# A bound and a skipped key in the second stage's row gathers of a two-layer graph network

## The chip, the cores and the metric

The kernel runs on one core of one Trainium2 chip. The metric is the device time of one execution in microseconds (us). The unchanged kernel took 4383.87 us as the median of 3 runs (4382.24 to 4384.48).

## The reference

N = 12500 nodes with D = 256 features (float32). Of the edge lists `src` and `dst`, 100000 drawn pairs stand in both directions (200000 edges) and 12500 self-loops are added; all 212500 are sorted by `dst`.

```python
# layer 1 (GIN with batch norm)
agg = segment_sum(x[src], dst, N)
z = (1 + eps_gin) * x + agg
z = relu(z @ W1 + b1) @ W2 + b2
z = (z - mean(z, 0)) * rsqrt(var(z, 0) + 1e-5) * gamma + beta
x = layernorm(x + (z + x))
# layer 2 (weighted graph convolution)
support = segment_sum(edge_weight[:, None] * x[dst], src, N)
x = layernorm(x + relu(support @ weight))
```

The first layer sums by `dst`, by which the edges are sorted. The second sums by `src`, by which they are not sorted.

## The kernel before, in words

The nodes are tiles of 128 rows (98 of them), the edges are pairs of chunks: a pair is 256 edges, 831 pairs in all. The function `gnn` holds one block of code for each engine; they work at the same time and meet at semaphores.

**First stage** (to about 2160 us of the span). POOL fetches the rows of x by indirect DMA, one DMA for 128 edges (`gather`, L552), into a ring of 32 pairs. DVE makes one-hot matrices from `dst`; PE multiplies the ring's rows by them and sums a node tile in PSUM, then the two dense layers follow. Beside this work the edges are sorted into 49 buckets of 256 nodes of `src` for the second stage: DVE works out each edge's place, PE packs the edges (`pack`, L1366) into runs of 64 slots, each slot a key and a weight. A slot that no edge takes holds key 0 and weight 0. ACT stores the runs in `stage_dram`. Self-loops don't go to a bucket; their weights go into a diagonal.

A **key** is `dst * 256 + (src mod 256)`: the row to fetch and the place in the bucket. The buckets' lists stand in a DRAM tensor `lists` of (key, weight), 4 + 4 bytes an entry. At the start of the kernel SP fills all of `lists` from the SBUF tile `zero_row` with 17 DMAs of 128 KB (L443), after a wait on `s_zero`, which DVE's `memset` of the tile raises (L653). `zero_row` is read as (key, weight) pairs, so that every entry begins as key 0, weight 0.

**Between the stages** (about 2160 to 2329 us) the batch norm and the first layer norm are applied, and x1 is written to `x1_dram` (12544 rows of 1 KB). POOL waits for the 17 fills and writes the runs to their places in `lists` by 47 indirect scatters (L590), in an order in which each run's empty slots are overwritten by the next run of its bucket; what is left of them stands behind a bucket's last entry. Each bucket is taken up to a whole number of pairs. POOL reads the lists back, 128 entries a row (L607), DVE takes the keys apart (L1138 to L1142: cast to integer, shift by 8 for the row to fetch, mask with 255 for the place), PE turns them round and ACT copies the result to `srcT` (indices), `dstT` (places) and `wT` (weights).

**Second stage** (from about 2329 us). POOL runs `rounds2` turns over the ring. For every two pairs there is an `If` on the number of pairs, a wait for the ring's places on `s_added2`, and four calls of `gather2` (L618), each an indirect DMA of 128 rows of x1. SP counts the landed rows (`s_landed2`, wait at L528) and loads the next indices (L518). DVE makes a weighted one-hot of 128x256 for each chunk (L1154: place equal to the node, times the weight), PE multiplies and adds (L1493), two matmuls for each chunk of 128 entries, one for each node tile of the bucket, then the diagonal's part (L1514), the transposes (L1523), the dense layer (L1533), and DVE and ACT do the last layer norm; ACT stores the result.

The DMA instructions of POOL are executed by POOL: the profile shows each as an instruction with a duration of its own, and the landing of the rows apart from it.

The function of the second stage's gather before the change (L615 to L618):

```python
            def gather2(q, c):
                nc.gpsimd.indirect_dma_start(
                    out=ring[:, q, c, :], out_offset=None, in_=x1_dram,
                    in_offset=bass.IndirectOffsetOnAxis(ap=idx[:, q, c:c + 1], axis=0)).then_inc(s_row2[q // TWO], 16)
```

and the loop that calls it:

```python
            with pool.Fori(0, rounds2) as r:
                for h in range(2):
                    pool.wait_ge(s_idx2[h], r * 16 + 16)
                    stand(pool)
                    for q in range(h * HALF, (h + 1) * HALF, TWO):
                        ...
                        with pool.If(r * RING + q < pairs2):
                            pool.wait_ge(s_added2, r * RING + q + 2)
                            stand(pool)
                            for b in range(TWO):
                                for c in range(2):
                                    gather2(q + b, c)
```

Of the kernel before, what the change touches and what calls it, by code (L numbers as in the profile page):

```python
# [6 lines left out]
P = 128  # L7
# [7 lines left out]
TWO = 2  # L15
# [14 lines left out]
ALONE = 2 * TWO + BATCH  # L30
SLOTS = 64
BIG = 1 << 20
IN_RANGE = "the table's entries are clamped to the pairs of a sweep when they are computed"
IN_RANGE2 = "the buckets' chunks are counted from the edges, and all edges fill no more than these pairs"
NORM_EPS = 1e-5
# [19 lines left out]
def gnn(nc, x, src, dst, edge_weight, w1, b1, w2, b2, gamma, beta, eps_gin, w3, lists, stage_dram, z_dram, x1_dram, out):  # L55
# [7 lines left out]
    NT = -(-N // P)  # L63
# [21 lines left out]
    with ctx:  # L85
        def sb(name, shape, dt):
            return ctx.enter_context(nc.sbuf_tensor(name, shape, dt))

        def sem(name):
            return ctx.enter_context(nc.semaphore(name))  # L90
# [70 lines left out]
        zero_row = sb("zero_row", [P, D], f32)  # L161
        all_ones = work[:, 3200:3200 + P]
        idx = sb("idx", [P, RING, 2], i32)
# [178 lines left out]
        s_zero = sem("s_zero")  # L342
# [11 lines left out]
        s_row2 = [sem(f"s_row2_{g}") for g in range(RING // TWO)]  # L354
# [22 lines left out]
        def entry(eng, j):  # L377

            _, values = nc.values_load_multi_w_load_instructions(  # L379
                table[0:1, ds(j, 1), :].rearrange("a t f -> a (t f)"), engines=[eng.engine], min_val=0, max_val=MOST,  # L380
                skip_runtime_bounds_check_because=IN_RANGE)
            return values

        def entry2(eng, j):

            _, values = nc.values_load_multi_w_load_instructions(
                table2[0:1, ds(j, 1), :].rearrange("a t f -> a (t f)"), engines=[eng.engine], min_val=0, max_val=ROWS,
                skip_runtime_bounds_check_because=IN_RANGE2)
            return values
# [21 lines left out]
        def _(sp):  # L411
# [26 lines left out]
                sp.dma_start(idx[:, begin:(h + 1) * HALF, :], srcT[:, begin:(h + 1) * HALF, :]).then_inc(s_idx[h], 16)  # L438

            sp.dma_start(x_pair[:, 0, :, :], x[0:2 * P, :].rearrange("(t p) d -> p t d", p=P)).then_inc(s_x_pair, 16)  # L440
            sp.wait_ge(s_zero, 1)
            for b in range(ZEROS):
                sp.dma_start(lists[b * P * P:(b + 1) * P * P, :].rearrange("(p n) f -> p (n f)", p=P),  # L443
                             zero_row[:, :]).then_inc(s_zero_rows, 16)
# [93 lines left out]
        def _(pool):  # L538
            nc.gpsimd.memset(src_i[:, NB - 1, :], 0).then_inc(s_fill, 1)
            nc.gpsimd.memset(dst_i[:, NB - 1, :], BIG).then_inc(s_fill, 1)  # L540
            nc.gpsimd.memset(next_i[:, NB - 1, :], BIG).then_inc(s_fill, 1)
            nc.gpsimd.memset(w_f[:, NB - 1, :], 0.0).then_inc(s_fill, 1)
# [63 lines left out]
            for b in range(BLOCKS):  # L606
# [3 lines left out]
                    in_offset=bass.IndirectOffsetOnAxis(ap=chunk_row_i[:, b:b + 1], axis=0)).then_inc(s_rows2, 16)  # L610
# [6 lines left out]
            def gather2(q, c):  # L617
                nc.gpsimd.indirect_dma_start(  # L618
                    out=ring[:, q, c, :], out_offset=None, in_=x1_dram,
                    in_offset=bass.IndirectOffsetOnAxis(ap=idx[:, q, c:c + 1], axis=0)).then_inc(s_row2[q // TWO], 16)  # L620

            with pool.Fori(0, rounds2) as r:
                for h in range(2):
# [3 lines that stand above are left out]
                        if q == AHEAD:  # L627
                            pool.wait_ge(s_list2, N_LIST2)
# [6 lines that stand above are left out]
# [3 lines left out]
        def _(dve):  # L638
# [10 lines left out]
            def edge_dmas(count):  # L649
                rows, rest = divmod(count, PAIR)  # L650
                return 16 * ((rows // P > 0) + (rows % P > 0) + (rest > 0))

            nc.vector.memset(zero_row[:, :], 0.0).then_inc(s_zero, 1)  # L653
            dve.wait_ge(s_src, edge_dmas(E))
            nc.vector.tensor_copy(src_f[:, :, :], src_i[:, :, :]).then_inc(s_cast, 1)
            dve.wait_ge(s_iota, 6)
# [101 lines left out]
            def after(k, n):  # L758

                dve.wait_ge(s_sort, k * (MEMBER_OPS + PLACE_OPS) + n)  # L760
                stand(dve)

            def members(k):
# [6 lines left out]
                nc.vector.tensor_scalar(local_i[:, :], src_k, BUCKET - 1, None, ALU.bitwise_and).then_inc(s_sort, 1)  # L770
                nc.vector.tensor_scalar(pad[:, :], dst_k, float(BIG), None, ALU.is_ge).then_inc(s_sort, 1)
                after(k, 3)
# [118 lines left out]
            def ones_of_tile(j, bank):  # L891

                new, head, m4, m2, _, _, _, shared, off, sweep = entry(dve, j)
                counted = sweep * RING + off
                base = tile_base[:, j:j + 1] if isinstance(j, int) else tile_base[:, ds(j, 1)]

                def equal(to, at, n):
                    at = nc.s_assert_within(at, 0, ROWS - n, skip_runtime_bounds_check_because=IN_RANGE)
                    return nc.vector.scalar_tensor_tensor(  # L899
                        out=to.rearrange("p b c n -> p (b c) n"),  # L900
                        in0=p_iota.unsqueeze(1).to_broadcast([P, 2 * n, P]), scalar=base,
                        in1=dstT[:, ds(at, n), :].rearrange("p b c -> p (b c)").unsqueeze(2).to_broadcast([P, 2 * n, P]),
                        op0=ALU.add, op1=ALU.is_equal)

                if not (isinstance(j, int) and j < 2):
                    dve.wait_ge(s_acc, j - 1)
                    stand(dve)
                equal(shared_of[bank], shared, 1).then_inc(s_onehot, 1)
                with dve.If(new < m4):
                    with dve.Fori(new, m4, 2 * TWO) as p:  # L910
                        for b in range(0, 2 * TWO, TWO):
                            dve.wait_ge(s_added, p + counted + (TILE_ONES + b - TWO))
                            stand(dve)
                            equal(loop_of[:, b:b + TWO], p + b, TWO).then_inc(s_onehot, TWO)
                with dve.If(m4 < head):
                    dve.wait_ge(s_added, m4 + counted + (TILE_ONES - TWO))
                    stand(dve)
                    equal(loop_of[:, 0:TWO], m4, TWO).then_inc(s_onehot, TWO)
                equal(heads_of[bank], head, BATCH)
                equal(last_of[bank], m2, 1).then_inc(s_onehot, TILE_ONES - 1)  # L920
# [310 lines left out]
        def _(pe):  # L1231
# [37 lines left out]
            def sum_tile(j, bank, others):  # L1269

                new, head, m4, m2, end, low, rep, _, off, sweep = entry(pe, j)
                first = sweep * RING
                counted = first + off
# [606 lines left out]
```

## Time and profile before

| what | value |
|---|---|
| median of 3 runs | 4383.87 us (4382.24 to 4384.48) |
| the profiled execution's own time | 4377.4 us |
| its span | 4374.5 us |
| PE busy | 3432.7 us (78%) |
| DVE busy | 2605.9 us (60%) |
| ACT busy | 411.9 us (9%) |
| POOL busy | 3195.1 us (73%) |
| DMA | 540.19 MB, mean 123 GB/s |
| mean granted TensorE clock | 0.903 of full speed |

How to read it: busy time is the time in which an engine has an instruction in work; register, branch and semaphore instructions are not counted. PE is TensorE, DVE is VectorE, ACT ScalarE, POOL GpSimd, SP SyncE. PEld is the weight load that goes with a matmul. An engine's name with a q (SPq, PEq) is its sequencer. L618 is line 618 of the kernel. "<-issue" is idle time in which the engine waited for nothing that the profile shows. The profiled execution is one run of its own, 6.5 us shorter than the median of the three.

### The profile page before, as it was taken

Reading aid. Unit: us, or ns where it says so; the run is one execution under the profiler, and the core shown is the slowest. Engines: PE = TensorE matmul, PEld = TensorE weight load, DVE = VectorE, ACT = ScalarE, POOL = GpSimd, SP = SyncE. Lnnn points to the kernel's source line nnn. Section 1 sums busy time; section 2 is a strip of 40 time slices with the busy share of each in tenths; the row PEclk is TensorE's granted clock in tenths of the full one; section 3 lists DMA queues with packets and bytes.
Section 4 is the critical chain, followed back from the end, with each engine's and each line's share of the span. In section 5 each row is a group of like instructions: output and inputs, shape, how many; then the busy total and the mean of one; then the engine's idle time right before and its main releaser. Section 6 shows DMA issues by size and latency. Waiting matters only on the chain.

```text
span 4374.5 us, 69588 instructions
## 1 busy us (share of the span) xinstructions
PE 3432.7 (78%) x16131; PEld 2823.7 (65%) x16132; DVE 2605.9 (60%) x5746; ACT 411.9 (9%) x1055; POOL 3195.1 (73%) x3456
## 2 busy tenths in 40 slices
PE   2788787877778787877636888888888888888887
PEld 2666676766666676766435666676666666666666
DVE  3888787877878787877474344344344344343343
ACT  0000000000000000000151000000000000000001
POOL 6777777777777777777345777777777777777775
PEclk7888888888888898889758999999999999999998
DMA  5344444444444444444583344434434344434343
GB/s 146 112 123 116 121 118 118 118 119 120 116 121 116 121 115 121 118 119 119 161 292 111 113 115 120 119 115 120 120 115 120 117 118 119 120 114 120 114 120 99
DMA packets 305380, 540.19 MB, mean 123 GB/s; under 512 B 85290, under 2 KB 197790, under 8 KB 305326
## 3 DMA queue, kind: packets, MB, share of 16 engines
q0 software_dynamic: 159424, 434.52, 34.5%
q10 hardware_dynamic: 89348, 67.77, 5.0%
q1 hardware_dynamic: 56554, 37.24, 2.9%
q8 instruction: 26, 0.43, 0.0%
q14 instruction: 28, 0.23, 0.0%
HBM read 489.80 MB, written 46.88 MB: 123 GB/s over the span
## 4 chain that ended last, share of the span: by engine, by line
POOL 34%; issue 27%; DVE 24%; DVEq 6%; PE 3%; DMA 2%; ACT 1%; POOLq 1%; ACTq 1%; SPq 0%; PEldq 0%
POOL ring L618 32%; DVE work L887 5%; DVEq L379 5%; DVE slot_is L881 3%; DVE work L784 2%; DVE ps L809 2%; DVE place_f L813 2%; POOL ring L552 1%; PE ps L1493 1%; DVE ones_sb L899 1%; DVE work L884 1%; DMA x_dram<-ring 1%; PE ps L1283 1%; DMA ring<-x_dram,idx 1%; DVE zstats L926 1%
## 5 line engine op out<-in xcount | busy, mean ns | idle before, releaser
L552 POOL DMA_INDIRECT ring<-in_x,idx x1664 | 1586.4, 953 | 503.7 <-issue 473.3
L618 POOL DMA_INDIRECT ring<-x_dram,idx x1612 | 1524.1, 945 | 521.0 <-issue 489.5
L1493 PE MATMUL ps<-ring,work 128*128 x6448 | 1527.1, 392 | 334.3 <-SPq L528 332.1
L1493 PEld LDWEIGHTS ps<-ring,work 128*128 128x128 f32 x6448 | 1221.7, 194 | 625.0 <-issue 465.6
L1154 DVE TENSOR_SCALAR work<-ps,dstT,wT 128x256 f32<-128x256 f32 x1612 | 741.8, 534 | 1136.0 <-PE ps L1493 1065.7
L1283 PE MATMUL ps<-ring,ones_sb 128*128 x3324 | 899.2, 418 | 133.4 <-DVE ones_sb L899 71.4
L1283 PEld LDWEIGHTS ps<-ring,ones_sb 128*128 128x128 f32 x3324 | 676.2, 210 | 286.1 <-issue 186.3
L899 DVE SCALAR_TENSOR_TENSOR ones_sb<-ps,tile_base,dstT 128x256 f32<-128x256 f32 (+1 forms) x294 | 316.1, 1103 | 219.2 <-issue 205.7
L1366 PEld LDWEIGHTS ps<-work 128*128 128x128 f32 x3384 | 414.6, 191 | 14.6 <-DVE work L887 2.3
L1366 PE MATMUL ps<-work 128*128 128x128 f32 x3384 | 415.8, 274 | 1.4 <-DVE work L887 1.4
L1293 PE MATMUL ps<-ring,ones_sb 128*128 x384 | 152.7, 536 | 233.8 <-DVE ones_sb L899 217.5
L884 DVE TENSOR_TENSOR work<-ps,current 128x768 f32<-128x768 f32 x282 | 266.6, 946 | 0.0
L887 DVE TENSOR_TENSOR work<-slot_is,ps 128x768 f32<-128x768 f32 x282 | 265.6, 942 | 0.0
L1293 PEld LDWEIGHTS ps<-ring,ones_sb 128*128 128x128 f32 x384 | 88.0, 254 | 264.1 <-issue 252.5
L1623 ACT ACTIVATE z_pair<-ps,cols 128x256 f32 (+1 forms) x98 | 41.2, 471 | 1496.6 <-DVE zstats L926 1451.9
L1784 ACT ACTIVATE work<-ps 128x512 f32<-128x512 f32 x49 | 29.3, 597 | 1446.9 <-PE ps L1523 1446.9
L881 DVE TENSOR_TENSOR slot_is<-ps,current 128x384 f32<-128x384 f32 x282 | 154.8, 549 | 6.7
L590 POOL DMA_INDIRECT lists<-work,target x47 | 45.5, 967 | 113.2 <-DMA lists<-work,target 71.9
L809 DVE TENSOR_TENSOR ps<-ps,work 128x588 f32<-128x588 f32 x141 | 109.7, 778 | 21.4 <-DVE place_f L813 0.5
L813 DVE TENSOR_REDUCE place_f<-ps 128x12 f32<-128x588 f32 x141 | 108.7, 771 | 20.6
L1346 PE MATMUL ps<-hidT,w2s 128*128 128x256 f32 x392 | 115.5, 424 | 3.8 <-ACT hidT L1613 3.8
L1450 PE MATMUL ps<-ident,ones_sb 128*128 128x128 f32 x196 | 48.0, 426 | 83.8 <-DVE ones_sb L1077 68.9
(244 smaller groups left out, 2160.2 us busy)
## 6 DMA issues: line engine op xcount, KB each, us to landing
ring<-in_x,idx POOLq DMA_INDIRECT x1664
ring<-x_dram,idx POOLq DMA_INDIRECT x1612, 2.7
z_dram<-z_pair ACTq DMA_DIRECT2D x49, 256.0 KB, 3.1
ones_sb<-x_dram ACTq DMA_DIRECT2D x49, 256.0 KB
ring<-z_dram SPq DMA_DIRECT2D x24, 512.0 KB, 6.0
ring<-in_x SPq DMA_DIRECT2D x24, 512.0 KB, 7.0
x_dram<-ring ACTq DMA_DIRECT2D x24, 512.0 KB, 4.3
out<-ones_sb ACTq DMA_DIRECT2D x48, 256.0 KB
```

The source lines that it names most:

```text
L379: _, values = nc.values_load_multi_w_load_instructions(table[0:1, ds(j, 1), :].rearrange("a t f -> a (t f)"), engines=[eng.engine], min_va ...
L552: nc.gpsimd.indirect_dma_start(out=ring[:, q, c, :], out_offset=None, in_=x, in_offset=bass.IndirectOffsetOnAxis(ap=idx[:, q, c:c + 1], ax ...
L618: nc.gpsimd.indirect_dma_start(out=ring[:, q, c, :], out_offset=None, in_=x1_dram, in_offset=bass.IndirectOffsetOnAxis(ap=idx[:, q, c:c + ...
L881: nc.vector.tensor_tensor(slot_is[:, q % 2, :, :], p_iota[:, 0:SLOTS].unsqueeze(1).to_broadcast([P, WIDTH, SLOTS]), current[:, 1, mine].un ...
L884: nc.vector.tensor_tensor(of_run[:, q, :, :], p_iota.unsqueeze(1).to_broadcast([P, WIDTH, P]), current[:, 0, mine].unsqueeze(2).to_broadca ...
L887: nc.vector.tensor_tensor(values[:, q, :, :, :], slot_is[:, q % 2, :, :].unsqueeze(3).to_broadcast([P, WIDTH, SLOTS, 2]), p_packed[:, :, m ...
L899: return nc.vector.scalar_tensor_tensor(out=to.rearrange("p b c n -> p (b c) n"), in0=p_iota.unsqueeze(1).to_broadcast([P, 2 * n, P]), sca ...
L1154: last = nc.vector.tensor_scalar(to[:, b, c, :], bucket_nodes, dstT[:, ds(at + b, 1), c], wT[:, ds(at + b, 1), c], ALU.is_equal, ALU.mult)
L1283: last = nc.tensor.matmul(wide, ones_of[:, b, c, :], summands[:, ds((p + b) & (RING - 1), 1), c, :].rearrange("p a d -> p (a d)"), start=F ...
L1293: nc.tensor.matmul(wide, shared_of[bank][:, 0, c, :], summands[:, ds((new + (RING - 1)) & (RING - 1), 1), c, :].rearrange("p a d -> p (a d)"),
L1366: last = nc.tensor.matmul(p_pack, of_run[:, q, c, :], values[:, q, c, :, :].rearrange("p n f -> p (n f)"), start=(q == 0 and c == 0), stop ...
L1493: last = nc.tensor.matmul(to[:, t * D:(t + 1) * D], ones_of[:, b, c, t * P:(t + 1) * P], ring[:, ds((p + b) & (RING - 1), 1), c, :].rearra ...
```

## The change

The fill of `lists` begins with a key beyond all nodes, 2^23 (row 2^23 / 256 = 32768), at weight 0: `zero_row` is written by two strided memsets in place of one, and SP waits for both. The second stage's gathers get a bound, the last row of `x1_dram` (12543), and indices above it are passed over without an error; nothing is written to the ring's row for them. The first stage's gathers, the scatters and the gathers of the lists stay as they are.

```diff
+NOBODY = 1 << 23
...
-            sp.wait_ge(s_zero, 1)
+            sp.wait_ge(s_zero, 2)
...
             def gather2(q, c):
                 nc.gpsimd.indirect_dma_start(
                     out=ring[:, q, c, :], out_offset=None, in_=x1_dram,
-                    in_offset=bass.IndirectOffsetOnAxis(ap=idx[:, q, c:c + 1], axis=0)).then_inc(s_row2[q // TWO], 16)
+                    in_offset=bass.IndirectOffsetOnAxis(ap=idx[:, q, c:c + 1], axis=0),
+                    bounds_check=NT * P - 1, oob_is_err=False).then_inc(s_row2[q // TWO], 16)
...
-            nc.vector.memset(zero_row[:, :], 0.0).then_inc(s_zero, 1)
+            nc.vector.memset(zero_row[:, :].rearrange("p (n f) -> p n f", f=2)[:, :, 0], float(NOBODY)).then_inc(s_zero, 1)
+            nc.vector.memset(zero_row[:, :].rearrange("p (n f) -> p n f", f=2)[:, :, 1], 0.0).then_inc(s_zero, 1)
```

## Rows read from the trace of the kernel before

**Rows 1.** Busy time by stretch (start:end, length, then each engine), whole span

```profile
100.00:2160.00 2060.00, 1650.59 (x8488) 1389.57 (x8487) 1620.74 (x3295) 163.60 (x522) 1545.29 (x1703) 0.87 0.42 118
2160.00:2330.00 170.00, 67.47 (x286) 54.60 (x284) 111.39 (x394) 89.84 (x177) 57.78 (x60) 0.56 0.80 264
2400.00:4374.00 1974.00, 1642.85 (x7067) 1322.74 (x7067) 803.46 (x1883) 148.80 (x338) 1470.22 (x1556) 0.98 0.40 117
```

**Rows 2.** The chain that ended last, shares by engine and by line

```profile
POOL 34%; issue 27%; DVE 24%; DVEq 6%; PE 3%; DMA 2%; ACT 1%; POOLq 1%; ACTq 1%; SPq 0%; PEldq 0%
POOL ring L618 32%; DVE work L887 5%; DVEq L379 5%; DVE slot_is L881 3%; DVE work L784 2%; DVE ps L809 2%; DVE place_f L813 2%; POOL ring L552 1%; PE ps L1493 1%; DVE ones_sb L899 1%; DVE work L884 1%; DMA x_dram<-ring 1%; PE ps L1283 1%; DMA ring<-x_dram,idx 1%; DVE zstats L926 1%
```

**Rows 3.** Groups on POOL: count, busy us, mean ns, idle before and its releasers

```profile
L552 POOL DMA_INDIRECT ring<-in_x,idx x1664 | 1586.4, 953 | 503.7 <-issue 473.3 <-PE ps L1283 12.1 <-DMA idx<-in_src 4.1
L618 POOL DMA_INDIRECT ring<-x_dram,idx x1612 | 1524.1, 945 | 521.0 <-issue 489.5 <-PEq L1556 30.3 <-PE ps L1493 1.2
L590 POOL DMA_INDIRECT lists<-work,target x47 | 45.5, 967 | 113.2 <-DMA lists<-work,target 71.9 <-DMA work<-stage_dram 39.4 <-issue 1.8
...
L607 POOL DMA_INDIRECT work<-lists,chunk_row_i x14 | 13.6, 974 | 10.0 <-DMA lists<-work,target 6.0 <-issue 4.0
...
L544 POOL IOTA part_i<- 128x1 int32 x1 | 0.1, 123 | 0.1
```

**Rows 4.** Waits from 2329 us on: total us, times, longest us

```profile
DVE work L1154 <- PE ps L1493: 1065.7, 117, 22.8
POOL ring L618 <- issue: 489.5, 1607, 0.3
...
PE ps L1493 <- SPq L528: 332.1, 306, 5.6
```

**Rows 5.** POOL's timeline at the stage's beginning: start us, duration us

```profile
2329.10 0.94 POOL L618 DMA_INDIRECT ring<-x_dram,idx  x1 [30.29 <-PEq L1556]
2330.35 0.94 POOL L618 DMA_INDIRECT ring<-x_dram,idx  x1 [0.30 <-issue]
2331.60 0.95 POOL L618 DMA_INDIRECT ring<-x_dram,idx  x1 [0.30 <-issue]
2332.85 0.95 POOL L618 DMA_INDIRECT ring<-x_dram,idx  x1 [0.30 <-issue]
2334.10 0.95 POOL L618 DMA_INDIRECT ring<-x_dram,idx  x1 [0.30 <-issue]
```

**Rows 6.** Chain at the end of the span: start us, us, what

```profile
4341.70 0.94 POOL ring L618
4342.64 0.30 issue
4342.95 3.57 DMA ring<-x_dram,idx
4346.55 0.32 issue
4346.87 3.72 PE ps L1493 x16
...
4370.10 1.09 ACT ones_sb L1795 x2
```

**Rows 7.** Busy time of the gathers' stretch: PE, PEld, DVE, ACT, POOL, clock, DMA share

```profile
2329.00:4344.00 2015.00, 1681.08 (x7235) 1353.72 (x7236) 829.74 (x1932) 142.14 (x324) 1524.06 (x1612) 0.98 0.40 117
```

**Rows 8.** Timeline of the first 30 us: DVE's first two instructions, SP's fill

```profile
0.87 0.27 DVE L653 MEMSET zero_row<- 128x256 f32 x1 [0.73 <-PEq L1860]
...
8.68 1.09 DVE L655 CAST ring<-ring 128x1792 f32<-128x1792 int32 x1 [7.53 <-DMA ring<-in_src]
...
20.16 9.08 SPq L443 DMA_DIRECT2D lists<-zero_row  x17
```

**Rows 9.** The gathers of line 618: ns min/median/max, and us to landing

```profile
L618 POOL DMA_INDIRECT ring<-x_dram,idx x1612: 942/946/958, 2329.1 to 4342.9; - x180
...
DMA to landing us min/median/max: 2.6/2.7/3.9
```

**Rows 10.** POOL's DMA queue: packets, MB, share of 16 engines' span

```profile
q0 software_dynamic: 159424, 434.52, 34.5%
```

## The prediction

> **What bounds the kernel now.** I read the table of stretches first. From 2330 us on the second stage runs at one mix to the end, and the span splits into 2160 us of first stage, 170 us between, and this last part [rows 1]. The diff touches gathers of this last part only, so that part decides. The chain that ended last gives POOL's line L618, which is the second stage's gather, 32% of the span, the largest share by far, and "issue" 27% [rows 2].
>
> Next, POOL's own groups. L618 is 1612 gathers of 945 ns each, 1524.1 us, and the idle time before them is 489.5 us of "issue" [rows 3]. The waits show that 1607 of the 1612 gathers waited for nothing that the profile shows, never more than 0.3 us, while PE waited 332.1 us for landed rows and DVE 1065.7 us for PE [rows 4]. So POOL feeds everybody and is fed late by nobody. The single gathers show the beat: one starts every 1.25 us from 2329.10 [rows 5] to 4342.95 [rows 6]. 4343.9 - 2329.1 = 2014.8 us, and / 1612 = 1.250 us per gather, with no gap in between. **Whatever the change does to one gather's time on POOL is multiplied by 1612**: 1 ns is 1.6 us. PE is busy 1681 us of these 2015 us, DVE 830, and the DMA engines have a share of 0.40 [rows 7], so none of them limits, and a POOL that is faster by a few per cent would still be the bound.
>
> What is left after the last gather is some 30 us of landing, sums and norms [rows 6], which the change doesn't touch but for the landing.
>
> **The change, part by part.**
>
> *The fill's two memsets.* Before, one memset of 128x256 at 0.87 us, 272 ns; then DVE stands until the edges land at 8.68 us. SP asks for the fill only at 20.2 us [rows 8]. Two strided ones of half the size each, even at 272 ns apiece, end before 1.5 us. Cost 0: hidden under DVE's wait of 7.5 us; without that cover it would be 0.3 us. SP waits for a count of 2 in place of 1, true 18 us before it asks; behind that wait stand only the 17 fills, the same in number and size. POOL waits for all the fills ahead of its first scatter, in the stretch from 2160 us on [rows 1], long after.
>
> *The key.* Keys become whole numbers by the same casts, shifts and transposes: nothing added. The padding's weight stays 0, so what lies in the ring from earlier is multiplied by 0; PE and DVE do the same work.
>
> *How many rows are passed over.* 1612 gathers of 128 entries are 206336. The reference draws 200000 edges (the 12500 loops go another way, as a diagonal); counted by bucket on the drawn lists, 199986 of them are no loops, so 6350 entries are padding. Not all keep the new key: a sorted run is written in pieces of 64 slots, and its empty slots hold key 0, a valid index. Following the runs of the last groups, 2167 padding entries at the buckets' ends get key 0 from a run's tail and 4183 keep the new key. These 4183 (2.0%) lie in 55 of the 1612 gathers; 19 gathers are passed over as a whole. The other 1557 gathers only carry the bound.
>
> *What passing over saves.* No row shows a gather with fewer rows, so bounds: a gather's 945 ns over its 128 rows is 7.4 ns, so at most 4183 x 7.4 = 31 us; at least 0, if a row left out takes POOL as long as a row described. POOL's smallest instruction, over 128x1, is 123 ns [rows 3], so some of the 945 is fixed: (945 - 123) / 128 = 6.4 ns, 27 us. I take 10 us, nearer to the lower end, since the gathers take 942 to 958 ns whatever their indices are [rows 9], padding chunks included, and since an index left out must still be read and judged. The Trainium skill speaks against the saving here ("DMA: Bandwidth & Descriptors", section "Anatomy of one DMA — SWDGE (gpsimd) path"): generating descriptors is a small part, and many can be emitted before the incremental cost shows; by it the saving would be about 0.
>
> *The DMA side.* 4183 rows of 1 KB are 4.3 MB less of 434.52 MB on the software queue [rows 10]. At a share of 0.40 this frees nothing that is waited for. The last gather took 3.57 us to land [rows 6] against a median of 2.7 us [rows 9], and its bucket ends in padding: at most 0.9 us gained, inside the 10 us.
>
> *What the bound costs on the sequencer.* If a register has to be loaded per gather, it falls in the time in which POOL works at the gather before. Each fourth gather already has a comparison, an addition and a wait ahead of it, and the gaps are 0.30 us there too [rows 4, 5]. So 0; without that cover, no row prices it.
>
> *What the bound costs in the gather itself.* This is the term that decides, and no row of before has a bound. Lower end: 0, if every index is compared today anyway or the comparison fits in free slots (I see no way for it to gain on a gather that leaves nothing out). Upper end: a pass of its own over the 128 indices, the price of POOL's smallest instruction, 123 ns. Nearest rows: the kernel's other forms of this same instruction, the scatter at 967 ns and the gather of the lists' chunks at 974 ns against 945 [rows 3]: another form of the work differs by 22 to 29 ns. I take 22 ns, of the group with more members.
>
> **Sum.** 1612 x 22 ns = +35.5 us, less 10 us: +25.5 us. The profiled execution took 4377.4 us (span 4374.5), so 4402.9; the median of the runs shown is 6.5 us above it, so **4409 us** (+0.6%).
>
> **The rivals.** A measurement of this kernel can tell about 0.2% (8.8 us) from no change.
>
> *A, the forecast: the check costs some tens of ns per gather, more than the skipping gives back.* For it: every ns counts 1612 times, from 12 ns up it loses more than 0.2% (12 x 1.612 - 10 = 9 us), and POOL now works from index to descriptor in 7.4 ns, so that any further step per index shows. Against: the step may run in parallel. Chance 0.36, of which 0.05 ends within 0.2%.
>
> *B, nothing moves.* The compare is free and leaving out saves nothing, or the bound isn't acted on at all (the change would not do what it says; a key of 2^23 is row 32768, beyond the 12544 rows). For it: the durations lie within 16 ns and show no dependence on the indices [rows 9]. 4384 us. Chance 0.29.
>
> *C, faster.* The check is free and a row left out saves its share: 27 to 31 us, with the tail up to 0.9 us more: 4353 to 4357 us; with a third of it, 4374. It needs a check under about 10 ns and a saving per row above 2.1 ns (8.8 / 4183). For it: POOL is the bound with no cover at all, so that each saved ns counts in full. Against: 1557 gathers pay, 55 earn. Chance 0.22.
>
> *D, clearly slower: judging each index is a separate step in POOL.* Its place is each gather of L618; its price is from 123 ns (a pass, above) to 822 ns (the whole present work of an index done twice, 945 - 123), thus 1612 x 0.123 - 10 = +188 us, 4572 us, up to +1315 us, about 5700 us. PE doesn't cover any of it, since it waits for POOL already. It decides from 12 ns on. Against: a loop at 7.4 ns per row leaves little room for such code to be slow. Chance 0.13. The Trainium skill has a rule of this kind ("GPSIMD Engine Reference", section "Elementwise — side-by-side cycle accounting"): data-dependent branching on this engine costs about 12 cycles per element; at the 1.2 GHz of the example there that would be an estimated 1.28 us per gather and over 6400 us. No row here shows it; 7.4 ns per row with an index read in it speak against it having applied so far.
>
> **How the numbers follow.** The likeliest case is A, 4409. Faster: C but for 0.01 within 0.2%, so 0.21. Same: B 0.29, 0.05 of A, 0.01 of C: 0.35. Slower: 0.31 of A and D's 0.13: 0.44. The range begins at 4354, nearly the full saving of C, and goes to 4550, beyond A with 100 ns per gather (+151 us, 4535); most of D and the last of C are left out, 0.12 together. As both signs hold weight: A's own range is 4385 to 4470.
>
> **What would show it.** In the changed kernel's profile L618's mean must be read: 967 ns or so by A with the beat at 1.27 us and the same 0.30 us of issue; 945 by B; by C 945 in most gathers and a lower minimum, in the 55 with padding; by D 1068 or more. The beat times 1612 must give the change of the span; if the mean stays and the gap grows, the cost is the sequencer's and my cover was wrong. The packets and MB of the software queue must fall by 4.3 MB, or the bound isn't acted on. The first stage (L552 at 953 ns, until 2160 us) must stay as it is. The forecast is wrong if the mean of L618 stays within 5 ns of 945, or goes beyond 1040.

## The result and the profile after

The changed kernel takes **4465.75 us** (median of 4 runs, 4462.17 to 4468.01) against 4383.2 us before (4 runs): a ratio of 1.0187 with a 95% interval of 1.0173 to 1.0202. It is 82.5 us slower. The direction was forecast, and the cause by name; the size was not: the sum had come to 25.5 us more. The profiled execution took 4462.17 us, with a span of 4459.1 us. Four of the experiments (`r3_bound_only`, `r3_hoist`, `e7_first_stage`, `e6_err`) ran beside a kernel before of 4376.94 us, as here, and all others beside one of 5424 to 5501 us, slowed, at a mean granted clock of about 0.82 in place of 0.90; each time is compared with the kernel before beside it.

POOL's groups on the changed kernel (line numbers have moved by one: L619 is L618 of before, L553 is L552) answer to [rows 3]:

```profile
L619 POOL DMA_INDIRECT ring<-x_dram,idx x1612 | 1612.9, 1001 | 521.1 <-issue 489.7 <-PEq L1559 30.5 <-PE ps L1496 0.9
L553 POOL DMA_INDIRECT ring<-in_x,idx x1664 | 1587.6, 954 | 504.3 <-issue 472.8 <-PE ps L1286 12.9 <-DMA idx<-in_src 3.9
```

The second stage's gather has gone from a mean of 945 to 1001 ns; the first stage's, which the diff leaves alone, from 953 to 954. The idle time before the 1612 gathers is the same to 0.1 us. The list of that line, which answers to [rows 9], shows what was added and how even the step is:

```profile
L619 POOLq MOVE  x1612: 29/29/29, 2327.2 to 4414.6; - x180
L619 POOL DMA_INDIRECT ring<-x_dram,idx x1612: 995/1002/1016, 2328.0 to 4430.6; - x180
```

The bound is a constant in the source and a register in the program: POOL's sequencer loads it anew for each gather, 29 ns. The shortest of the 1612 gathers is 995 ns long, the longest before was 958: every gather has become longer, also the 1557 that pass nothing over. The timeline (answers to [rows 5]) has the new beat with the old gap:

```profile
2328.02 1.01 POOL L619 DMA_INDIRECT ring<-x_dram,idx  x1 [30.47 <-PEq L1559]
2329.34 1.01 POOL L619 DMA_INDIRECT ring<-x_dram,idx  x1 [0.31 <-issue]
2330.65 1.00 POOL L619 DMA_INDIRECT ring<-x_dram,idx  x1 [0.30 <-issue]
```

The last gather starts at 4430.58 and takes 1.00 us, so the beat is (4431.58 - 2328.02) / 1612 = 1.305 us against 1.250: 55 ns. **Where the time came from:** 1612 x 55 = 88.7 us in the second stage; the stage began 1.1 us earlier; and the tail behind the last gather, 30.6 us before, is 27.5 us. 88.7 - 1.1 - 3.1 = 84.5 us; the spans differ by 84.6. Most of the shorter tail can be named on the chain that ended last, which answers to [rows 6]:

```profile
4430.58 2.27 DMA ring<-x_dram,idx
4432.89 0.32 issue
4433.21 3.72 PE ps L1496 x16
...
4440.21 1.96 PE ps L1536 x8
```

The last gather's rows landed after 2.27 us in place of 3.57; by a count on the drawn lists, 114 of its 128 entries are passed over. This 1.3 us is all that the passing over gave: in the four experiments beside 4376.94 us the last landing takes 3.58 to 3.62 us in the three kernels that keep key 0, and 2.27 us in the one with the new key. The next 1.6 us are in a group of eight matmuls of the dense layer, 1.96 us in place of 3.54; it is 1.96 us with the bound alone as well, so it has nothing to do with the passed rows, and its cause is open. The rest of the machine had slack, as said (the row answers to [rows 7]):

```profile
2328.00:4432.00 2104.00, 1681.42 (x7237) 1350.85 (x7238) 832.43 (x1931) 142.14 (x324) 1612.92 (x1612) 0.98 0.37 111
```

PE's 1681 us of work and DVE's 832 now spread over 2104 us. At the start, the two memsets are as cheap as forecast and lie in the same wait of DVE [rows 8]:

```profile
L444 SPq DMA_DIRECT2D lists<-zero_row x17: 428/461/660, 21.2 to 29.6; - x17
L655 DVE MEMSET zero_row<- x1: 165/165/165, 0.9 to 0.9; 128x128 f32 x1
L656 DVE MEMSET zero_row<- x1: 165/165/165, 1.0 to 1.0; 128x128 f32 x1
```

**Did it pass rows over?** The page's line of DMA packets and that of POOL's queue, changed kernel:

```profile
DMA packets 305382, 536.89 MB, mean 120 GB/s; under 512 B 86080, under 2 KB 198596, under 8 KB 305327
...
q0 software_dynamic: 159424, 431.21, 33.4%
```

434.52 - 431.21 = 3.31 MB, or 3232 rows of 1 KB (0.01 MB of rounding is 10 rows). So it did, but fewer than the 4183 that I had counted. A second count on the drawn lists that puts every run at its place in the order of the scatters gives 3241 entries with the new key (3.32 MB), in 55 gathers, none of them wholly passed over. The first count followed only the empty slots behind the last runs. The runs of the first 23 groups are laid right-aligned, with their empty slots in front, and those of the next bucket reach back into the last chunk of a padded bucket: not all empty slots that are left stand behind a bucket's last entry, as the words on the kernel before had it. The number of packets, 159424, is unchanged [rows 10]: a row that is passed over does not shorten the queue's list, it makes a packet small.

### The profile page after: what moved, and what is told of

The parts are those of the page before. It is cut to its first block, busy times and chain, and to the rows that moved or that the text cites. A ratio compares the mean times of both kernels' runs of the same rounds, so it can differ in the third digit from the quotient of the medians.

```text
span 4459.1 us, 71201 instructions
## 1 busy us (share of the span) xinstructions
PE 3438.7 (77%) x16131; PEld 2824.9 (63%) x16132; DVE 2613.1 (59%) x5747; ACT 411.8 (9%) x1055; POOL 3285.3 (74%) x3456
## 3 DMA queue, kind: packets, MB, share of 16 engines
q0 software_dynamic: 159424, 431.21, 33.4%
HBM read 489.80 MB, written 46.88 MB: 120 GB/s over the span
## 4 chain that ended last, share of the span: by engine, by line
issue 34%; POOL 30%; DVE 23%; DVEq 6%; DMA 2%; PE 2%; POOLq 2%; ACT 1%; ACTq 0%; SPq 0%; PEldq 0%
POOL ring L619 27%; DVE work L890 5%; DVEq L380 4%; POOL ring L553 3%; DVE slot_is L884 2%; DVE work L787 2%; DVE ps L812 2%; DVE place_f L816 2%; DVE ones_sb L902 1%; DMA x_dram<-ring 1%; DVE work L887 1%; PE ps L1286 1%; POOLq L619 1%; PE ps L1496 1%; DVE zstats L929 1%
## 5 line engine op out<-in xcount | busy, mean ns | idle before, releaser
L619 POOL DMA_INDIRECT ring<-x_dram,idx x1612 | 1612.9, 1001 | 521.1 <-issue 489.7
L553 POOL DMA_INDIRECT ring<-in_x,idx x1664 | 1587.6, 954 | 504.3 <-issue 472.8
L1496 PE MATMUL ps<-ring,work 128*128 x6448 | 1526.8, 391 | 421.2 <-SPq L529 419.5
```

The source lines that it names most:

```text
L553: nc.gpsimd.indirect_dma_start(out=ring[:, q, c, :], out_offset=None, in_=x, in_offset=bass.IndirectOffsetOnAxis(ap=idx[:, q, c:c + 1], ax ...
L619: nc.gpsimd.indirect_dma_start(out=ring[:, q, c, :], out_offset=None, in_=x1_dram, in_offset=bass.IndirectOffsetOnAxis(ap=idx[:, q, c:c + ...
L1496: last = nc.tensor.matmul(to[:, t * D:(t + 1) * D], ones_of[:, b, c, t * P:(t + 1) * P], ring[:, ds((p + b) & (RING - 1), 1), c, :].rearra ...
```

## The experiments

**The bound alone.** The lists are filled with key 0 as before, only the bound is added:

```diff
-                    in_offset=bass.IndirectOffsetOnAxis(ap=idx[:, q, c:c + 1], axis=0)).then_inc(s_row2[q // TWO], 16)
+                    in_offset=bass.IndirectOffsetOnAxis(ap=idx[:, q, c:c + 1], axis=0),
+                    bounds_check=NT * P - 1, oob_is_err=False).then_inc(s_row2[q // TWO], 16)
```

> The kernel before with the bound alone: the lists are filled with key 0 again, so no index is beyond the bound and no row is passed over. Theory G (having a bound costs, passing over is free and saves nothing): 1001 ns a gather, 4466 us. Theory S (the skipped rows cost the time): 945 ns and 4384 us. Theory V (the bound costs more than the 56 ns seen and the skipping gave some of it back): a mean above 1001 ns, and up to 3241 rows x 6.4 ns = 21 us more, 4487 us.

> The bound alone (lists filled with key 0, no row passed over), timed again in the hope of a chip on which POOL is the bound of the second stage, as on the first. There, theory G (the bound is the whole cost): 1612 x 54 ns = 87 us more than the kernel before, 4466 to 4471 us, +1.9%. Theory S (passing over rows is the cost): 4384 us. On a chip on which POOL waits for TensorE: the gather 999 ns again and the time within 0.5% of the kernel before.

These two are the same kernel, and `e2_bound_only` is told with the last experiment. Beside 4376.94 us, `r3_bound_only` gave 4461.51 us (4 runs), a ratio of 1.0192 (1.0175 to 1.0209), the same as the whole change. The profile of that run:

```profile
L618 POOL DMA_INDIRECT ring<-x_dram,idx x1612 | 1612.8, 1000 | 522.5 <-issue 489.1 <-PEq L1557 31.8 <-PE ps L1494 1.5
```

```profile
DMA packets 305381, 540.20 MB, mean 121 GB/s; under 512 B 85290, under 2 KB 197790, under 8 KB 305326
...
q0 software_dynamic: 159424, 434.52, 33.6%
```

1000 ns a gather, and not one row passed over (434.52 MB). So the bound is the whole cost within the interval, and the skipped rows are none of it and give nothing back but the 1.3 us in the last landing. The packets under 512 B are 790 fewer than in the changed kernel; 789 groups of four neighbouring entries, by the second count, hold only the new key, so such a group fits to one packet left nearly empty.

**The bound in a register, once.** The changed kernel with

```diff
+            last_row = nc.alloc_register(nc.gpsimd.engine, "last_row")
+            nc.gpsimd.reg_mov(last_row, NT * P - 1)
...
-                    bounds_check=NT * P - 1, oob_is_err=False).then_inc(s_row2[q // TWO], 16)
+                    bounds_check=last_row, oob_is_err=False).then_inc(s_row2[q // TWO], 16)
```

> The changed kernel with the bound moved into a register once, ahead of the loop, in place of one move of 29 ns before each of the 1612 gathers. Theory R (the register move is part of what the longer gather shows): the gather's mean falls from 1001 ns by about 29 ns, the time by 1612 x 29 = 47 us to about 4419 us. Theory G (the gather itself works longer once it carries a bound; the move is hidden behind the gather before): 1001 ns and 4466 us as before, and the 1612 moves are gone from the trace.

> The changed kernel with the bound in a register once, beside it. On a chip on which POOL is the bound: the same +1.9% if the moves of 29 ns are hidden behind the gather before (their removal took nothing off the gap of 0.30 us), +0.8% (4419 us) if they are not.

```profile
L622 POOL DMA_INDIRECT ring<-x_dram,idx x1612 | 1612.8, 1000 | 523.5 <-issue 490.1 <-PEq L1562 32.9 <-PE ps L1499 0.6
```

The 1612 moves are gone, the gather is 1000 ns, the idle time 490.1 us of "issue" as ever, and the time 4461.6 us (4 runs, ratio 1.0191, 1.0174 to 1.0208), beside 1.0192 for the bound alone with its moves. A move of 29 ns ahead of each gather costs nothing as long as POOL still works at the gather before. Theory R falls.

**Half of the rows passed over, and nearly all.** On the kernel with the bound alone:

```diff
-                    bounds_check=NT * P - 1, oob_is_err=False).then_inc(s_row2[q // TWO], 16)
+                    bounds_check=NT * P // 2 - 1, oob_is_err=False).then_inc(s_row2[q // TWO], 16)
```

> As the kernel with the bound alone, but the bound is the middle row (6271), so that about half of all rows are passed over; left out: their share of the second sum. If a row passed over saves POOL its share of a gather, 64 rows x 6.4 ns = 410 ns, the gather takes about 590 ns and the second stage becomes bound by TensorE, 1680 us in place of 2104, in all about 4050 us. If it saves nothing: 1001 ns and 4466 us, with the software queue's MB down by a quarter. If leaving out costs, above 1001 ns.

> Bound 0, so that nearly every row of the second stage's gathers is passed over; left out: the second sum but for node 0's rows. Theory G: 1001 ns still, the software queue's MB down by about half (206 MB), the time on a chip bound by POOL the same. If a whole gather passed over is shorter (a way out that half a gather doesn't take): clearly below 945 ns.

For the second the bound is 0. In each fence the first line is the gather's group, the second the queue's; half of the rows, then nearly all:

```profile
L618 POOL DMA_INDIRECT ring<-x_dram,idx x1612 | 1607.7, 997 | 842.0 <-issue 462.7 <-remote 254.3 <-PE ps L1494 80.7
...
q0 software_dynamic: 159424, 333.19, 21.6%
```

```profile
L618 POOL DMA_INDIRECT ring<-x_dram,idx x1612 | 1612.5, 1000 | 854.1 <-issue 460.3 <-remote 262.2 <-PE ps L1494 87.8
...
q0 software_dynamic: 159424, 230.55, 15.6%
```

With nearly all rows left out 204 MB fewer are moved, and the gather is as long as with none left out. Passing rows over saves POOL nothing, whether 3241 rows or some 200000. Each is one run on a slowed chip (5455.66 and 5473.72 us, where before took 5423.86 and 5501.49), so of these runs the gather's length is what counts: it hardly changes with the chip's condition (997 to 1001 ns in all nine profiles of 128 rows with this silent bound; the first stage's gathers without one 950 to 956 ns in all profiles). With the bound 0 the trace has no move at all ahead of the gathers, and they take 1000 ns all the same.

**Fewer rows in a gather, without and with the bound.** In the kernel before, and in the one with the bound alone, `out=ring[0:P // 2, q, c, :]` and `ap=idx[0:P // 2, q, c:c + 1]` in place of all 128 partitions, and the same with `P // 4`:

> The kernel before with gathers of 64 rows in place of 128 in the second stage, without a bound; left out: the rows of the upper 64 partitions. It shows how much of the 945 ns goes with the rows. If only the 123 ns of POOL's smallest instruction are fixed: 123 + 64 x 6.4 = 534 ns. If a gather is mostly fixed work: above 800 ns.

> Gathers of 64 rows with the bound; left out: the rows of the upper 64 partitions. It goes with the gathers of 64 rows without a bound, 901 ns. Theory F (a fixed step per instruction, as reading the register or another path through the descriptor code): 901 + 54 = 955 ns. Theory I (a comparison per index, 56 / 128 = 0.44 ns each): 901 + 28 = 929 ns.

> Gathers of 32 rows without a bound; left out: the rows of the upper 96 partitions. From 945 ns at 128 rows and 901 at 64 a line gives 857 ns fixed and 0.69 ns a row: 879 ns at 32 rows. If the length doesn't follow the rows on a line (steps of a whole group of partitions), another value.

> Gathers of 32 rows with the bound; left out: the rows of the upper 96 partitions. With the bound 1000 ns at 128 rows and 938 at 64 give 876 ns fixed and 0.97 ns a row: 907 ns at 32 rows, so that the bound would cost 28 ns there, 19 of them fixed and 0.28 for each row. If the bound is a fixed step after all: 879 + 54 = 933 ns. If all of it goes by rows: 879 + 14 = 893 ns.

The four groups, in that order, one kernel each:

```profile
L618 POOL DMA_INDIRECT ring<-x_dram,idx x1612 | 1452.5, 901 | 993.6 <-issue 498.4 <-remote 327.9 <-PE ps L1493 125.6
```

```profile
L618 POOL DMA_INDIRECT ring<-x_dram,idx x1612 | 1512.0, 938 | 973.0 <-issue 507.0 <-remote 351.4 <-PE ps L1494 71.4
```

```profile
L618 POOL DMA_INDIRECT ring<-x_dram,idx x1612 | 1390.6, 863 | 1077.5 <-issue 495.0 <-remote 373.1 <-PE ps L1493 166.3
```

```profile
L618 POOL DMA_INDIRECT ring<-x_dram,idx x1612 | 1456.1, 903 | 1026.7 <-issue 503.7 <-remote 318.4 <-PE ps L1494 159.2
```

| rows in a gather | without a bound | with it | the bound costs |
|---|---|---|---|
| 128 | 945 ns | 1000 ns | 55 ns |
| 64 | 901 ns | 938 ns | 37 ns |
| 32 | 863 ns | 903 ns | 40 ns |

The runs of 64 and 32 rows are one each and on slowed chips; the first stage's gathers there take 951 to 954 ns, as ever. With 64 rows and the bound, neither theory met its value: 938 ns lie between 929 (all by rows) and 955 (all fixed). Both expectations for 32 rows missed as well: without a bound 863 where a line gave 879, and the bound 40 ns where the split "19 fixed, 0.28 a row" gave 28. Two things stand. A gather is mostly a fixed piece of work: with a quarter of the rows it still takes 91% of the time, so that the 7.4 ns a row of my bound were ten times too much (44 ns for 64 rows is 0.7 ns a row). And most of what the bound costs doesn't go with the rows either: 37 to 40 of the 55 ns are there at half and at a quarter of the rows (the 3 ns between them are no more than one kernel's mean moves from run to run). How the remaining 15 to 18 ns come in between 64 and 128 rows stays open.

**An index beyond the bound as an error.** `oob_is_err=True` on the kernel with the bound alone; no index is beyond it.

> The bound alone, but with an index beyond it counted as an error (none is). If the 54 ns belong to comparing with a bound: 999 ns again. If they belong to the silent passing over: about 945 ns.

```profile
L618 POOL DMA_INDIRECT ring<-x_dram,idx x1612 | 1629.9, 1011 | 521.9 <-issue 489.1 <-PEq L1557 31.0 <-PE ps L1494 1.8
```

1011 ns and 4486.27 us (one run; before 4376.94). The form that reports is 11 ns dearer still than the silent one; the mean's 66 ns x 1612 are 106 us, and 109 were measured. So the cost is not that of being silent. Neither value in the expectation was met exactly; the nearer one, that comparing costs, holds.

**The bound on the first stage's gathers in place of the second's.**

```diff
-                    in_offset=bass.IndirectOffsetOnAxis(ap=idx[:, q, c:c + 1], axis=0)).then_inc(s_gathered[q // QUARTER], 16)
+                    in_offset=bass.IndirectOffsetOnAxis(ap=idx[:, q, c:c + 1], axis=0),
+                    bounds_check=N - 1, oob_is_err=False).then_inc(s_gathered[q // QUARTER], 16)
```

> The bound (last node) on the first stage's 1664 gathers in place of the second's; no index is beyond it. The gather there should go from 953 to about 1008 ns. Where its beat of 1.25 us and the copies of the self weights set the pace of the first stage, 1664 x 55 ns = 92 us come on top, 4475 us; if DVE, busy 1621 of 2060 us there, is level with POOL, all of the 92 us still shows, since POOL is in front of both; if DVE is ahead as the limit, less than half of it.

```profile
L552 POOL DMA_INDIRECT ring<-in_x,idx x1664 | 1676.7, 1008 | 504.1 <-issue 473.7 <-PE ps L1284 11.1 <-DMA idx<-in_src 4.6
L619 POOL DMA_INDIRECT ring<-x_dram,idx x1612 | 1528.0, 948 | 518.0 <-issue 490.8 <-PEq L1557 26.9 <-PE ps L1494 0.3
L591 POOL DMA_INDIRECT lists<-work,target x47 | 45.7, 972 | 96.2 <-DMA lists<-work,target 73.0 <-DMA work<-stage_dram 21.4 <-issue 1.8
```

953 became 1008 ns, the same step, and the last gather of the stage starts 92.0 us later (2207.4 against 2115.4). The time is 4450.33 us (one run): 73 us more, so neither all of the 92 us, as the first two cases of the expectation had it, nor less than half. The first gather of the second stage starts 70.2 us later (2399.3 against 2329.1), so 22 us found cover between the stages: the idle time before the scatters is 96.2 us in place of 113.2 [rows 3], mostly because the wait for the runs to be read back has shrunk from 39.4 to 21.4 us, and the wait before the second stage 26.9 in place of 30.3. The second stage then takes 4.3 us longer, at 948 ns a gather. POOL is the bound in the first stage too, but what it loses there is partly covered in the step between the stages. In the second stage nothing follows that could give such cover.

**The changed kernel and the bound alone, again, on a slowed chip.**

> The changed kernel once more, beside the kernel before on the same chip, since the chip of the first four experiments ran both kernels a quarter slower at a lower granted clock, with POOL waiting for other engines. On a chip where POOL is the bound both theories expect +1.9% again and 1001 ns a gather; on a chip where POOL waits in the second stage, most of the 56 ns is hidden in those waits, and less than +0.6% is left.

> The bound alone with the lists filled by key 0, beside the changed kernel on the same chip. Theory G (the bound is all of the cost; rows passed over neither save nor cost): the same time as the changed kernel within 0.2%, both on the chip of the first result and on this one. Theory V (skipping gives something back): up to 64 / 44 ns measured per row of difference in the gather of 64 rows, that is 3241 rows x 0.7 ns = 2 us longer than the changed kernel, below what can be told.

Changed: 5506.83 us against 5501.49, ratio 1.0006 (0.9981 to 1.0031); the bound alone 5511.04 us, 1.0014 (0.9984 to 1.0045). Beside before at 5423.86 us, `e2_bound_only` gave 5446.48 us, 1.0046 (1.0026 to 1.0066), and `e1_hoist`, with the register, 5430.24 us, 1.0012 (0.9989 to 1.0035). The gathers of the changed kernel there:

```profile
L619 POOL DMA_INDIRECT ring<-x_dram,idx x1612 | 1612.5, 1000 | 863.9 <-issue 463.1 <-remote 255.1 <-PE ps L1496 97.9
```

and the second stage's stretch:

```profile
2974.00:5403.00 2429.00, 1802.72 (x7012) 1433.26 (x7012) 815.09 (x1867) 140.03 (x317) 1612.39 (x1612) 0.85 0.32 96
```

and PE's group of the second sum:

```profile
L1496 PE MATMUL ps<-ring,work 128*128 x6448 | 1690.2, 417 | 526.9 <-issue 399.8 <-DVE work L1157 122.7 <-SPq L529 1.0
```

The gather is 1000 ns again, but POOL is idle for 864 us before its gathers in place of 521: it waits 97.9 us for PE and 255.1 us for something that the trace can't name ("remote"). PE waits 1.0 us for landed rows, where it waits 419.5 us in the changed kernel's first profile, and the span goes on for 82 us after the last gather, where it was 27.5 us: POOL is not what this stage waits for. The stage takes 2429 us, and hardly any of the 55 ns more a gather is left in the time. That they went into POOL's waits is argued, since no profile of the kernel before was taken in this condition. The same bound costs 1.9% where POOL is the limit and 0.1 to 0.5% where it has to wait.

## Why the prediction was right in direction and wrong in size

- **That POOL is the bound of the second stage, with no cover, so that each ns on a gather counts 1612 times:** right. 55 ns of beat made 88.7 us of stage.
- **The memsets and the later wait of SP at 0:** right (165 ns each, in DVE's wait).
- **The register on the sequencer at 0:** right, and shown: there is a move of 29 ns for each gather, and without the moves nothing gets faster.
- **The bound in the gather, taken at 22 ns between 0 and 123:** this is the step that failed. It measured 55 ns. These 33 ns are 53 us of the 57 that were missing. The ends held it; the choice by "the nearest row", the difference between forms of the instruction, was a guess about resemblance: neither the scatter (967 ns) nor the gather of the lists (974 ns) carries a bound, so they say nothing of its price, and the second has a mean of 950 to 975 ns from profile to profile, over its 14 gathers. The middle of the ends, about 61 ns, would have been nearer, but for no better reason. Why a bound takes 55 ns is still not known; the runs show only that it is not the register's move, not the passed rows, and for the most part not a price for each row.
- **What passing over saves, taken at 10 us between 0 and 31:** wrong. It was 0 in the gathers, and 1.3 us in the last landing. The upper end took a gather's time as a time per row; it is mostly fixed. The Trainium skill's statement, in "DMA: Bandwidth & Descriptors" (section "Anatomy of one DMA — SWDGE (gpsimd) path"), that many descriptors can be emitted before the incremental cost shows, agrees with 945 against 863 ns for four times the rows. It was weighed and should have had the sum. With both terms mended, 1612 x 55 - 1.3 = +87 us, against 84.6 in the spans of the two profiles and 82.5 in the medians; the earlier start of the stage (1.1 us) and the 1.6 us in the tail make up the first difference.
- **How many rows:** 4183 forecast and 19 gathers wholly passed over, against 3241 by the second count (3232 by the traffic) and none; the empty slots in front of the next bucket's first runs were forgotten. It changed nothing in the time.
- **The DMA side frees nothing that is waited for:** right for the 3.31 MB, but for the 1.3 us in the last landing. The runs that move up to 204 MB less don't test it, since POOL was not the limit there.
- **Rival B (nothing moves)** is out by 1.0173, the lower end of the interval. **Rival C (faster)** fell on both of its conditions. **Rival D** began at 123 ns a gather; 55 lie between A and it, nearer to A. The estimate from the Trainium skill's rule of about 12 cycles per element for data-dependent branching ("GPSIMD Engine Reference", section "Elementwise — side-by-side cycle accounting"), 1.28 us a gather, did not come true: 55 ns over 128 rows are 0.4 ns a row.
- **The range** reached to 4550 and A's own to 4470, and the result of 4466 lies inside both; the forecast value is what missed, by 57 us.

## What to carry to other kernels

A bound on an indirect gather is not free on the engine that issues it (55 ns on 945 here), and the rows that it passes over save traffic only: it costs where the issuing engine is the limit, and could pay only where DMA traffic is, which no run here shows. What should shorten such a stage is fewer gathers, not emptier ones, since a gather of 32 rows took 863 ns of the 945; leaving out a wholly padded chunk's gather would by this be worth a beat of 1.25 us each, an estimate that wasn't tried here. And before a price is taken between two ends far apart, ask whether the row that it is taken from has the same kind of work in it at all.

## What the runs showed of the hardware that was not expected

- The length of an indirect gather hardly depends on its rows: 863, 901 and 945 ns for 32, 64 and 128 rows of 1 KB, and shows no dependence on how many of them are passed over (997 to 1001 ns for none to nearly all, with a bound).
- A bound that reports costs more than one that is silent, 1011 against 1000 ns, with no index beyond it in either.
- A row passed over leaves its place in a packet: 159424 packets on the queue with 434.52, 431.21, 333.19 and 230.55 MB.
- The page's line of HBM traffic says 489.80 MB read in all of these, so it can't serve to tell whether rows were passed over; the queue's MB can. It does fall, to 384.15 and 331.33 MB, when the gathers list only 64 and 32 rows: it goes by the rows listed, passed over or not.
- The same kernel took 4377 and 5424 us at two times on what is named as the same chip, at mean granted clocks of about 0.90 and 0.82. What the extra 1050 us are spent on is open: no profile of it was taken at 5424 us, and in the other kernels' traces of that condition the waits on "remote" have no releaser.
